# Gates of a mixture of experts over hidden channels: from transposes in the last feed-forward to rows read back from memory

## The reference, cut to what matters

```python
shared = (silu(x @ sw_gate) * (x @ sw_up)) @ sw_down
probs = softmax(x @ router_w.T)
top_w, top_i = top_k(probs, 2)
top_w = top_w / sum(top_w)
combine = sum(one_hot(top_i, 8) * top_w[..., None], axis=1)      # 2048 tokens x 8
h = silu(einsum('th,ehi->eti', x, w_gate)) * einsum('th,ehi->eti', x, w_up)
routed = einsum('eth,te->th', einsum('eti,eih->eth', h, w_down), combine)
return routed + sigmoid(x @ shared_gate_w)[:, None] * shared
```

## Time and profile before

| | us |
|---|---|
| median of 3 runs | 5424.44 |
| lowest and highest run | 5420.89, 5425.71 |
| span of the profiled execution | 5423.2 |
| PE busy in it | 5193.4 (96%) |
| DVE, ACT, POOL busy | 3246.3, 2765.4, 1900.2 |

### The profile page before, as it was taken

How to read it: one execution, slowest core, us unless ns; L and a number is a source line. 1 busy time by engine, 2 the same in 40 slices (tenths; PEclk the granted TensorE clock), 3 DMA queues, 4 the chain that set the end, 5 groups by cost and what they waited for, 6 DMA issues and landing times. The chain is left out here.

```text
span 5423.2 us, 138613 instructions
## 1 busy us (share of the span) xinstructions
PE 5193.4 (96%) x58674; PEld 3455.6 (64%) x58674; DVE 3246.3 (60%) x7451; ACT 2765.4 (51%) x6000; POOL 1900.2 (35%) x2353
## 2 busy tenths in 40 slices
PE   6999999999999989999999999999898999999999
PEld 3666666666666665777777654333466677677565
DVE  6899999999999953444444338664444444444222
ACT  5888888888878832555555312666412222222111
POOL 4888888888888830000000002000000111111000
PEclk8999999999999989999999998999999999999999
DMA  1000000000000000000000000000101211221100
GB/s 32 7 8 12 7 8 7 8 7 7 12 7 25 3 2 12 13 11 15 13 11 11 26 0 8 1 1 1 63 1 42 69 62 69 69 68 62 54 4 8
DMA packets 34216, 114.60 MB, mean 21 GB/s; under 512 B 4416, under 2 KB 9792, under 8 KB 33600
## 3 DMA queue, kind: packets, MB, share of 16 engines
q1 hardware_dynamic: 33600, 105.74, 5.7%
HBM read 103.63 MB, written 2.10 MB: 19 GB/s over the span
## 5 line engine op out<-in xcount | busy, mean ns | idle before, releaser
L719 POOL TENSOR_TENSOR d_kq<-d_kq,d_tot 128x512 f32<-128x512 f32 x448 | 526.8, 1176 | 93.0 <-PE d_lpd L323 65.1
L825 DVE SCALAR_TENSOR_TENSOR d_qkv<-d_fr,d_wts,d_qkv 128x509 f32<-128x509 f32 (+2 forms) x576 | 427.3, 742 | 35.0 <-ACT d_qkv L663 16.0
L2019 DVE TENSOR_REDUCE r_nm<-r_ps 128x2 f32<-128x1024 f32 x256 | 307.6, 1222 | 141.8 <-PE r_ps L1838 141.7
L1240 POOL TENSOR_TENSOR f1rstd<-f1var,mhalf 128x4 f32<-128x4 f32 x4 | 4.0, 1010 | 1091.0 <-DVE f1var L1265 1091.0
L312 PE MATMUL d_fr<-xnT,d_wts 128*128 128x512 f32 x768 | 371.8, 608 | 11.2 <-DVE d_qkv L825 5.9
L2117 PE MATMUL e_pj<-xnT,e_wts 128*128 128x512 f32 x768 | 348.1, 603 | 11.7 <-DMA e_wts<-in_w3all 10.4
L1939 ACT ACTIVATE r_pT<-r_ps 128x512 f32<-128x512 f32 x512 | 274.9, 598 | 149.8 <-PE r_ps L1846 149.3
L723 POOL TENSOR_TENSOR d_kF<-d_kF,d_tot 128x256 f32<-128x256 f32 x448 | 305.8, 683 | 116.1 <-PE d_lpd L323 111.2
L1470 PEld LDWEIGHTS c_po<-c_pT,c_vt 128*128 128x128 f32 x2304 | 294.7, 191 | 21.0 <-ACT c_pT L1535 9.2
L1573 DVE TENSOR_TENSOR c_sc<-c_sc,c_mask 128x128 f32<-128x128 f32 x256 | 76.7, 300 | 383.2 <-PE c_sc L1425 383.2
L1470 PE MATMUL c_po<-c_pT,c_vt 128*128 128x128 f32 x2304 | 301.9, 276 | 0.2
(11 more groups left out here) (501 smaller groups left out, 13365.5 us busy)
## 6 DMA issues: line engine op xcount, KB each, us to landing
e_wts<-in_w3all SPq DMA_DIRECT2D x64, 897.0 KB, 4.5
d_wts<-in_headw SPq DMA_DIRECT2D x16, 583.5 KB, 3.8
c_wqo<-in_wqo SPq DMA_DIRECT2D x32, 256.0 KB, 2.6
f3ws<-in_f3w SPq DMA_DIRECT2D x17, 384.0 KB, 7.3
f2ws<-in_f2s SPq DMA_DIRECT2D x16, 256.0 KB, 6.2
f2qs<-in_f2q SPq DMA_DIRECT2D x16, 256.0 KB, 7.0
f1ws<-in_f1w SPq DMA_DIRECT2D x8, 384.0 KB, 6.4
f0w<-in_f0w SPq DMA_DIRECT2D x6, 384.0 KB, 5.8
```

The lines of the kernel that those rows point to most:

```text
L719: return nc.gpsimd.tensor_tensor(v, v, bc(bc(by_pair(u, lv)[:, :, 0], 2, h), 1, 2), ALU.mult)
L825: return nc.vector.scalar_tensor_tensor(into, fr[:, x // 2, 0:GRP - 3 + i], tap(u, x, i), into, ALU.mult, ALU.add)
L2019: nc.vector.tensor_reduce(nm[:, t % 2, half, 4 * j + i0:4 * j + i0 + 2], ps[:, row_pair(row - 1):row_pair(row - 1) + 2], AX, ALU.max).then ...
```

## The change

The gates are turned once, and not in each step. They are kept in one tile `T.g3` (experts, then the shared gate, by blocks of 128 tokens), of which `T.w3` is a view. In iteration 58 of the decay attention PE transposes it (9 x 16 columns, so a transpose of 128 and one of 16) into a slot of the `md` ring of its own, and DVE copies it out. In iteration 60 SP stores it to a tensor in device memory, `T.gates3`, of 9 rows by 2048 tokens.

In `feed_forward`, SP reads rows of that tensor back with each row repeated over the partitions: for the first 11 tiles of a group (the routed experts) into one of four buffers `gate`, one DMA for each expert that has channels in the tile (18 a group), for the six others one DMA a group into one of two buffers `shared`. A buffer is loaded again when DVE is done with the step four gated tiles ago. The first four tiles' gates are issued between the weight loads. The stores of the finished groups are issued in the same queue, after the gates of step 1 of the next group. DVE's first product takes `gate` or `shared` in place of `side`. `blocks`, `wide`, `side` and the work that fills them are gone from this stage.

```diff
@@ feed_forward
-BLK = 16
-EX, SH = 8 * 176 // BLK, 704 // BLK
-def feed_forward(nc, T, name, NTL, kind, w, weigh=None, blocks=None, prepare=None, raw=None, ternary=False, out=None, norms=NG):
+def feed_forward(nc, T, name, NTL, kind, w, weigh=None, spread_rows=None, prepare=None, raw=None, ternary=False, out=None, norms=NG):
...
-        side = psum("side", [P, 2, GRP]) if weigh or blocks is not None else None
+        side = psum("side", [P, 2, GRP]) if weigh else None
-        wide = sb("wide", [P, 3, NC, P]) if blocks is not None else None
+        gate = sb("gate", [P, 4, GRP]) if spread_rows is not None else None
+        shared = sb("shared", [P, 2, GRP]) if spread_rows is not None else None
...
+        gate_loaded = [sem(f"gate_loaded{i}") for i in range(4)]
+        shared_loaded = [sem(f"shared_loaded{i}") for i in range(2)]
+        ROUTED = NTL if spread_rows is None else max(t for t in range(NTL) if len(spread_rows(t)) > 1 or spread_rows(t)[0][0] < E3) + 1
+        gated = [n for n in range(TOTAL) if n % NTL < ROUTED]
...
+                def store(g):
+                    sp.wait_ge(added, g + 1)
+                    sp.dma_start(out.rearrange("(t p) d -> p t d", p=P)[:, g * NC:(g + 1) * NC], T.x[:, g * NC:(g + 1) * NC]).then_inc(stored, 16)
+
+                def gates_of(n):
+                    g, t = divmod(n, NTL)
+                    if t < ROUTED:
+                        i = gated.index(n)
+                        if i >= 4:
+                            sp.wait_ge(hid_ready, gated[i - 4] + 1)
+                        for e, r0, r1 in spread_rows(t):
+                            sp.dma_start(gate[r0:r1, i % 4], T.gates3[e:e + 1, g * GRP:(g + 1) * GRP].to_broadcast([r1 - r0, GRP])).then_inc(gate_loaded[i % 4], 16)
+                    elif t == ROUTED:
+                        if g >= 2:
+                            sp.wait_ge(hid_ready, (g - 1) * NTL)
+                        sp.dma_start(shared[:, g % 2], T.gates3[E3:E3 + 1, g * GRP:(g + 1) * GRP].to_broadcast([P, GRP])).then_inc(shared_loaded[g % 2], 16)
+
                 if raw is not None:
                     sp.dma_start(gs[:], raw[1]).then_inc(g_loaded, 16)
+                if spread_rows is not None:
+                    sp.wait_ge(T.gates_stored, 32)
                 for t in range(0 if ternary else NTL):
                     sp.dma_start(ws[:, t], w[t]).then_inc(loaded[t], 16)
                     if raw is not None:
                         sp.dma_start(qs[:, t], raw[0][t]).then_inc(loaded[t], 16)
+                    if spread_rows is not None and t < 4:
+                        gates_of(t)
+                if spread_rows is not None:
+                    for n in range(4, TOTAL):
+                        gates_of(n)
+                        if n % NTL == 1 and n > NTL:
+                            store(n // NTL - 1)
                 if out is not None:
-                    for g in range(NG):
-                        sp.wait_ge(added, g + 1)
-                        sp.dma_start(out.rearrange("(t p) d -> p t d", p=P)[:, g * NC:(g + 1) * NC], T.x[:, g * NC:(g + 1) * NC]).then_inc(stored, 16)
+                    store(NG - 1)
...
@@ feed_forward, PE
-                        if blocks is not None:
-                            pe.wait_ge(widened, n + 1)
                         for k in range(NC):
-                            column = weigh(g * NC + k, t) if weigh else wide[:, n % 3, k]
-                            last = nc.tensor.transpose(side[:, n % 2, k * P:(k + 1) * P], column, T.ident[:])
+                            last = nc.tensor.transpose(side[:, n % 2, k * P:(k + 1) * P], weigh(g * NC + k, t), T.ident[:])
...
@@ feed_forward, ACT
-                def widen(m):
-                    g, t = divmod(m, NTL)
-                    if m >= 3:
-                        act.wait_ge(wide_mm, m - 2)
-                    w8 = blocks[:, g * NC:(g + 1) * NC, t * P // BLK:(t + 1) * P // BLK]
-                    nc.scalar.activation(wide[:, m % 3].rearrange("p c (b i) -> p c b i", i=BLK), bc(w8, 3, BLK), ACT.Copy).then_inc(widened, 1)
-
-                if blocks is not None:
-                    act.wait_ge(expanded, 1)
-                    widen(0)
-                    widen(1)
...
-                    if blocks is not None and n + 2 < TOTAL:
-                        widen(n + 2)
...
@@ feed_forward, DVE
-                    nc.vector.tensor_copy(blocks[:, :, 0:EX].rearrange("p t (e c) -> p t e c", e=E3), bc(T.w3[:], 3, EX // E3))
-                    nc.vector.tensor_copy(blocks[:, :, EX:EX + SH], T.shared[:, :, 0:1].to_broadcast([P, NT, SH]))
-                    nc.vector.memset(blocks[:, :, EX + SH:], 0.0).then_inc(expanded, 1)
...
-                    if side is None:
+                    if spread_rows is not None:
+                        if t < ROUTED:
+                            i = gated.index(n)
+                            dve.wait_ge(gate_loaded[i % 4], sum(16 * len(spread_rows(m % NTL)) for m in gated[i % 4:i + 1:4]))
+                            over = gate[:, i % 4]
+                        else:
+                            dve.wait_ge(shared_loaded[g % 2], 16 * (g // 2) + 16)
+                            over = shared[:, g % 2]
+                        ch.link(nc.vector.tensor_tensor(h, act1[:, n % 2], over, ALU.mult))
+                        nc.vector.tensor_tensor(h, h, pg[:, n % 2, 1, :], ALU.mult).then_inc(hid_ready, 1)
+                    elif side is None:
                         nc.vector.tensor_tensor(h, act1[:, n % 2], pg[:, n % 2, 1, :], ALU.mult).then_inc(hid_ready, 1)
                     else:
                         dve.wait_ge(wide_mm, n + 1)
                         ch.link(nc.vector.tensor_tensor(h, act1[:, n % 2], side[:, n % 2, :], ALU.mult))
-                        nc.vector.tensor_tensor(h, h, act1[:, n % 2] if kind == "relu2" else pg[:, n % 2, 1, :], ALU.mult).then_inc(hid_ready, 1)
+                        nc.vector.tensor_tensor(h, h, act1[:, n % 2], ALU.mult).then_inc(hid_ready, 1)
...
@@ decay_attention
+        gates = sb("gates", [P, 2, P])
+        gates_ready = sem("gates_ready")
-        md_slot = lambda n: 4 * n + max(0, (n - 1) // NU3)
+        GATES = 3 * NU3 + 10
+        N_SLOTS = {g * NU3 + NU3 + 1: 1 for g in range(NGR)} | {GATES: 1}
+        further = lambda n: sum(c for at, c in N_SLOTS.items() if at <= n)
+        md_slot = lambda n: 4 * min(n, N) + further(n)
...
+                    if n == GATES + 2:
+                        rows = T.gates3.rearrange("e (t p) -> (e t) p", p=P)
+                        sp.wait_ge(md_read, md_slot(GATES))
+                        sp.dma_start(rows[0:P], gates[:, 0]).then_inc(T.gates_stored, 16)
+                        sp.dma_start(rows[P:P + NT], gates[0:NT, 1]).then_inc(T.gates_stored, 16)
...
+                    if n == GATES:
+                        pe.wait_ge(gates_ready, 1)
+                        m = into_mid()
+                        nc.tensor.transpose(md[:, m, 0:P], T.g3[:, 0:E3].rearrange("p e t -> p (e t)"), T.ident[:])
+                        nc.tensor.transpose(md[0:NT, m, P:2 * P], T.g3[:, E3], T.ident[:]).then_inc(md_mm, 1)
...
+                        if n == GATES:
+                            dve.wait_ge(md_mm, s0)
+                            nc.vector.tensor_copy(gates[:, 0], md[:, (s0 - 1) % 3, 0:P])
+                            nc.vector.tensor_copy(gates[0:NT, 1], md[0:NT, (s0 - 1) % 3, P:2 * P]).then_inc(md_read, 1)
...
-                        for copy in range(2):
-                            ch.did(nc.vector.tensor_scalar(T.shared[:, :, copy], zs[:], 0.5, 0.5, ALU.mult, ALU.add))
+                        ch.link(nc.vector.tensor_scalar(T.g3[:, E3], zs[:], 0.5, 0.5, ALU.mult, ALU.add))
+                        dve.sem_inc(gates_ready, 1)
...
@@ build_program, ffn3
-        T.w2, T.w3, T.shared = sb("w2", [P, NT, E2]), sb("w3", [P, NT, E3]), sb("shared", [P, NT, 2])
+        T.w2, T.g3 = sb("w2", [P, NT, E2]), sb("g3", [P, E3 + 1, NT])
+        T.w3 = T.g3[:, 0:E3].rearrange("p e t -> p t e")
...
+        T.gates3 = nc.dram_tensor("gates3", (E3 + 1, B * S), F32).ap()
+        T.gates_stored = nc.alloc_semaphore("gates_stored")
...
-    with nc.sbuf_tensor("f3_blocks", [P, NT, 17 * P // BLK], F32) as blocks:
-        feed_forward(nc, T, "f3", 17, "silu", ins["f3w"], blocks=blocks, out=T.out)
+    width = 176
+
+    def experts_of(t):
+        r0, r1 = t * P, (t + 1) * P
+        if r0 >= E3 * width:
+            return [(E3, 0, P)]
+        return [(e, max(r0, e * width) - r0, min(r1, (e + 1) * width) - r0) for e in range(E3) if e * width < r1 and (e + 1) * width > r0]
+
+    feed_forward(nc, T, "f3", 17, "silu", ins["f3w"], spread_rows=experts_of, out=T.out)
```

4 lines of the change are left out of this document (1 added, 3 removed).

## The result

| | before, us | changed, us |
|---|---|---|
| median | 5423.94 | 5394.31 |
| lowest and highest | 5420.89, 5425.71 | 5388.21, 5401.64 |
| runs | 4 | 4 |
| span of the profiled run | 5423.2 | 5399.8 |

The ratio is 0.9947, with a 95% interval of 0.9933 to 0.9961: 29.6 us less by the medians (forecast: 5395, 29 us less). The profiled run of the changed kernel took 5401.64 us, the longest of the four.

A forecast was written before the change was run, and what follows sets the result against it. PE's own work was taken to bound the last stage, without idle time. The span of 5423.2 less 29.9 plus 0.6 gives 5393.9 us, with 1.2 us to the median 5395.1; forecast's own range 5391 to 5398, overall 5391 to 5404.

The forecast's parts named there:

- The transposes: Last feed-forward: without them PE's step goes from 5.60 to 5.16 us, 29.9 us less over 68 steps.
- The decay attention: Iteration 58: two transposes take 0.22 us and PE stalls 0.3 to 0.5 us for DVE's copy, 0.6 us in all.
- The start of the stage: Last feed-forward: gate loads between and behind the weight loads delay them, gate tile 4 landing at 5053.3, at no cost.
- the 2.6 us that I had named as the limit: Start of the last stage: gate loads cost nothing as long as one gate tile takes under 2.6 us.
- The gates behind a store: Last stage: gates queued behind a store make DVE wait 2 to 3 us, three times; PE stalls only beyond 10.3 us.
- the late case: The rival "Late in places": gate loads of 4 us stall PE in the last stage, 5405 us; chance 0.10.
- The room of DVE: Last stage: DVE could be 5.5 us late before PE stalls, 5.1 us after the change.
- the limit of 5063.1: Start of the last stage: PE stalls only if gate tile 4 lands after 5063.1 us.
- Late in places: Rival, last stage: a gate load takes 4 us, PE stalls 7 us at the start and three times 1; 5405 us, chance 0.10.
- One after another: Rival, last stage: DMA engines fetch a gate tile's rows singly, 18.4 us a tile, 5927 us; chance 0.06.
- No shorter step: Rival, last stage: PE waits by what was taken out, or the step stays at 5.60 us; 5425 us, chance 0.04.

The follow-up runs named there:

- experiment 1: The changed kernel with four transposes of the identity, result unused, put back into each step of the last feed-forward: 5422.59 us, ratio to the kernel before 1.000.
- experiment 5: The changed kernel timed again without any edit, beside the kernel before on the same chip: 5394.72 us, ratio to the kernel before 0.9948.
- experiment 3: The changed kernel with gate loads of the same size reading 128 different rows of the stage's weights: 5392.28 us, ratio to the kernel before 0.9941.
- experiment 4: The changed kernel with six more 384 KB loads behind each of the three stores that have gates behind them: 5414.78 us, ratio to the kernel before 0.9984.
- experiment 6: The changed kernel with one gate buffer in place of four: 5400.28 us, ratio to the kernel before 0.9960.

## Why the prediction was right, step by step

**The transposes.** 29.9 us were forecast from steps of 5.60 and 5.16 us. The stage became 30.4 us shorter, with the step of 5.16 us; putting the transposes back restored 5.59 and all of the time. The half microsecond more lies in the first three steps: from PE's start to the first down products it is 14.5 us before and 12.7 after, 1.8 where three sets of transposes make 1.3. It is in the first eight products, which begin at a granted clock of 0.50 in both. Before, they take 6.35 us, from 5034.12 to

```profile
5040.47 0.60 PE L1184 MATMUL f3side<-ident,f3wide 128*128 128x128 f32 x4
```

and after, 5.81 (12.67 less two times 3.43), because the clock is back at 1.00 sooner after PE's start: it is 0.55 on average from 3.9 to 5.9 us after that start before (5038 to 5040), and 0.69 from 4.0 to 5.0 us after it, then 1.00, in the changed kernel (5045 to 5046). In experiment 1 they take 6.0 and in experiment 5 5.5 us, so this half microsecond is scatter and no part of the gain.

**The decay attention.** 0.6 us forecast, 0.51 measured in the trace, with its two parts (0.22, and 0.29 of the 0.3 to 0.5 us of waiting). In the whole it can't be told from the scatter of 4 us of that stage.

**The start of the stage.** The weights land and PE starts 4.79 us after the first issue (4.57 before), with gate loads between the weight loads, and no stall follows:

```profile
5036.24 0.33 SPq L1154 DMA_DIRECT2D f3ws<-in_f3w  x1
...
5041.03 12.83 PE L1200 MATMUL f3pg<-xnT,f3ws 128*128 128x512 f32 x24 [8.66 <-DMA f3ws<-in_f3w]
...
5042.08 7.97 SPq L1154 DMA_DIRECT2D f3ws<-in_f3w  x13
...
5053.70 1.89 PE L1176 MATMUL f3py<-f3ws,f3hid 128*128 128x256 f32 x8
```

I had worked with 399 GB/s for the gates. By themselves they move at less than half of that, about 1.6 us a tile at the 167 GB/s of experiment 3, which is within the 2.6 us that I had named as the limit. The gates of step 4 landed 26.0 us after the first issue, at 5062.2; the forecast had 23.8 (5053.3 less 5029.55). DVE wants them at 5064.85, so nothing waits. The rate of 103 GB/s in the Trainium skill (DMA: Bandwidth & Descriptors, section on latency and other measured facts), from which I had estimated 2.5 us, is for another pattern; the 142 to 167 GB/s here lie between it and the 399 of the earlier trace rows. That the same channel is the cause stays an inference: experiment 3 shows that it is where the loads read (one row of one tensor, against 128 rows of another), not why.

**The gates behind a store.** I had the gates of the next step at 6.8 to 8.1 us after DVE begins, DVE 2 to 3 us late three times, and some 2 us to spare before PE. DVE and SP after the first store, and PE:

```profile
5137.09 0.69 DVE L1304 TENSOR_TENSOR f3hid<-f3act,f3gate 128x512 f32<-128x512 f32 x1 [3.75 <-ACT f3act L1234]
...
5139.73 0.40 SPq L1134 DMA_DIRECT2D out<-x_res  x1
...
5145.47 0.69 DVE L1304 TENSOR_TENSOR f3hid<-f3act,f3gate 128x512 f32<-128x512 f32 x1 [5.76 <-DMA f3gate<-gates]
5146.20 0.69 DVE L1305 TENSOR_TENSOR f3hid<-f3hid,f3pg 128x512 f32<-128x512 f32 x1
...
5148.31 3.60 PE L1200 MATMUL f3pg<-xnT,f3ws 128*128 128x512 f32 x8
```

DVE begins at 5137.09 and gets the gates at 5145.4, 8.3 us later. It would have been ready at 5142.25, so it is 3.2 us late. PE's next up products that need this result start at 5148.31, without a gap. The result is there at 5146.89, 1.4 us before. So each of the three numbers was missed by a little, on the side of the late case: 8.3, 3.2 and 1.4 us. Who DVE waited for in the stage, us in total and times:

```profile
DVE f3hid L1304 <- ACT f3act L1234: 240.0, 65, 12.3
DVE f3hid L1304 <- DMA f3gate<-gates: 16.4, 3, 5.8
```

The waits for gates are 5.8 us long in the row because the time in which DVE would wait for ACT anyway is in them. One step of the working was wrong. The room of DVE is the time from the end of its product in step n to the up products of step n+2, and two steps lie in it, so the change takes 2 x 0.44 us off it and not 0.44: 5.5 - 0.9 = 4.6 us. The trace has just that (3.2 us late, 1.4 to spare), and so has experiment 4, in which DVE is 9.7 us late and PE 5.1. PE stalls beyond 9.8 us after DVE begins, not beyond 10.3. At the start the limit of 5063.1 was right, since it follows from 5067.2 less six times 0.44 and 1.4 us; it is DVE's own time there that was half a microsecond too early.

**The rivals.** "Late in places" was priced at what PE waits. Experiments 4 and 6 show that a stall of 5 us costs 7.5 to 7.7, because the clock falls. With 2.9 us more on the 7 us at the start, as in experiment 6, the case would have cost about 13 us, not 10 (an estimate). "One after another" did not happen: a gate tile of 256 KB by itself (`shared`) lands in 4.4 us, not 18.4. "No shorter step" did not either: the step is 5.16 us.

**The place of the time.** The median of 5394.31 is 0.8 us from the forecast, but that is luck in part. The runs lie from 5388 to 5402, wider than the 5391 to 5398 that I had given the forecast itself. I had taken the spread of three runs of the kernel before; 17 more on one chip went from 5411 to 5429. The terms that were off (the gates' rate, the room) were covered and so could not show in the time.

## What to carry to other kernels

When one engine is busy without a gap and another kernel or stage runs the same work without the part in question, the difference of the two steps, from start to start, is the gain to expect. Before putting work on another resource, work out by how much it may be late (here 4.6 us for DVE, counted over all the steps that lie between), and then look for what stands ahead of it in its queue, since a store in the same queue, with the issues behind it, made up more than half of the delay here. A load that is issued as late as it takes to land costs more than the idle time printed: one more buffer for the weights took 16.5 and 17.0 us off the decay attention, more than half of what the change gave.

## What the runs showed of the hardware

- A load that reads one row of 2 KB for 128 partitions takes 4.4 us to land where 128 different rows of that size, of another tensor, take 2.9. A run of the repeated loads moves 142 to 167 GB/s with the DMA engines busy for 0.89 and more of the time.
- After 4.9 us without work (experiment 4) PE's granted clock was 0.60 on average over the next 5.9 us (0.50 is 1.2 GHz), which cost 2.4 us on eight products; after 4.76 us in experiment 6 it was 0.54, which cost 2.9 us.
- Four transposes of 128x128 in f32 take 0.43 us of PE from start to start at a granted clock of 1.00, though each row of four says 0.60.
- The time of one program scatters by several us from run to run (5411 to 5429 on one chip). The decay attention's length went from 868.4 to 872.6 us over nine profiles with three weight buffers, and from 851.8 to 852.4 over four with four.
